# Delta rule in a new order on every engine, with its decays made in the gate stage

## The reference, cut to what matters

```python
qkvz = x @ W_in                              # x after layer norm
b, a = split(x @ W_ba, 2)
q, k, v = silu(causal_conv4(q, k, v))
beta = sigmoid(b);  g = -exp(max(A_log, -2.3)) * softplus(a + dt_bias)
q = l2norm(q) * 64 ** -0.5;  k = l2norm(k)
for each token t:                            # per sequence and head
    S = S * exp(g)
    S = S + k (v - k.T S) * beta
    y = q.T S
y = y * rsqrt(mean(y*y) + 1e-6) * norm_w * silu(z);  out = y @ W_o
```

## Time and profile before

| | |
|---|---|
| three runs | 5923.43, 5942.83, 5943.84 us; median 5942.83 |
| the profiled execution | 5944.53 us, its span 5942.7 us |
| granted TensorE clock, mean | 0.757 |
| TensorE, VectorE, GpSimd, ScalarE busy | 4563.3, 3452.1, 2243.2, 1849.6 us |
| gate stage | about 1475 to 1763 us |
| delta stage | 1763 to about 4960 us, with its start until 1930 |

### The profile page before, as it was taken

One profiled execution on the slowest core, in us unless ns is written; L12 is line 12 of the kernel. 1 busy time (PEld: TensorE's weight loads), 2 busy tenths in 40 slices (PEclk: granted clock), 3 DMA queues, 4 the chain that ended last, 5 costly groups with the idle time before them and its releaser, 6 DMA issues. The chain is left out here.

```text
span 5942.7 us, 161345 instructions
## 1 busy us (share of the span) xinstructions
PE 4563.3 (77%) x65093; PEld 3220.1 (54%) x65093; DVE 3452.1 (58%) x6879; ACT 1849.6 (31%) x3151; POOL 2243.2 (38%) x2773
## 2 busy tenths in 40 slices
PE   7888869997226888888888888888888875887544
PEld 6666634444223666666666666566666654666221
DVE  3444467876225666666666666666666543554577
ACT  0000011111224444444444444444444432333000
POOL 1111100000013666766666666666666651000000
PEclk6555579998556888888888888888888886555777
DMA  0000000000121111111111111111111110000210
GB/s 13 11 14 11 9 25 11 14 11 15 37 62 23 30 32 28 31 30 30 30 28 29 29 32 28 30 30 31 29 30 29 27 27 16 19 19 22 55 32 25
DMA packets 684989, 153.48 MB, mean 26 GB/s; under 512 B 560345, under 2 KB 674721, under 8 KB 683937
## 3 DMA queue, kind: packets, MB, share of 16 engines
q1 hardware_dynamic: 675872, 139.90, 12.1%
q10 hardware_dynamic: 8448, 4.20, 0.2%
HBM read 90.41 MB, written 53.50 MB: 24 GB/s over the span
## 5 line engine op out<-in xcount | busy, mean ns | idle before, releaser
L1604 DVE SCALAR_TENSOR_TENSOR d_acc<-d_xr,d_cq,d_acc 128x512 f32<-128x512 f32 x768 | 591.7, 771 | 164.0 <-ACT d_acc L1277 140.2
L1424 PE MATMUL d_pa<-d_wv,d_hs 128*128 128x512 f32 x1024 | 536.2, 672 | 0.0
L1246 POOL TENSOR_TENSOR d_prod<-d_tblk,d_ablk 128x15 f32<-128x15 f32 (+7 forms) x960 | 426.5, 444 | 114.1 <-DMA d_ablk<-a_blocks 33.8
L1399 PE MATMUL d_pa<-d_hq,d_wqk 128*128 128x259 f32 x1024 | 419.4, 549 | 47.4 <-ACT d_acc L1277 42.0
L1249 POOL TENSOR_TENSOR d_tblk<-d_tblk,d_prod 128x15 f32<-128x15 f32 (+7 forms) x960 | 420.1, 438 | 75.2
L1409 PE MATMUL d_pa<-d_kq 64*64 64x128 f32 x4096 | 182.4, 327 | 291.4 <-DVE d_qk L1620 221.0
L1276 ACT ACTIVATE d_xr<-d_pa 128x518 f32<-128x518 f32 x256 | 154.1, 602 | 767.1 <-PE d_pa L1399 765.5
L1424 PEld LDWEIGHTS d_pa<-d_wv,d_hs 128*128 128x128 f32 x1024 | 227.1, 227 | 241.0 <-issue 229.4
L1223 POOL TENSOR_TENSOR d_nr<-d_n,d_powers 128x32 f32<-128x32 f32 x64 | 347.4, 5428 | 5.9 <-DVE d_n L1734 5.9
L1409 PEld LDWEIGHTS d_pa<-d_kq 64*64 64x64 f32 x4096 | 146.1, 161 | 324.3 <-issue 324.3
L1219 POOL TENSOR_TENSOR d_f<-d_ms,d_mhalf 128x16 f32<-128x16 f32 x64 | 213.6, 3337 | 254.8 <-DVE d_ms L1653 254.8
(11 more groups left out here) (389 smaller groups left out, 10927.0 us busy)
## 6 DMA issues: line engine op xcount, KB each, us to landing
d_hs<-h_t SPq DMA_DIRECT2D x512, 32.0 KB, 1.8
t_blocks<-d_tblk SPq DMA_DIRECT2D x64, 256.0 KB, 2.0
a_blocks<-d_at SPq DMA_DIRECT2D x512, 16.0 KB, 1.8
d_ablk<-a_blocks SPq DMA_DIRECT2D x64, 128.0 KB, 2.1
d_ti<-t_blocks SPq DMA_DIRECT2D x512, 16.0 KB, 1.9
d_tt<-t_blocks SPq DMA_DIRECT2D x512, 16.0 KB, 1.9
d_hq<-h_t SPq DMA_DIRECT2D x16, 259.0 KB, 3.0
a_xt<-in_x SPq DMA_DIRECT2D x16, 256.0 KB, 2.9
```

The costliest lines, as they stand in the source:

```text
L1246: link(pool.tensor_tensor(prod[:, 0:s + 1, 0:n], tblk[:, 0, 0:s + 1, s].unsqueeze(2).to_broadcast([P, s + 1, n]), ablk[:, s, s + 1:SB].uns ...
L1399: last = pe.matmul(pa[:, A + b, 0:QH], wqk[:, col * P:(col + 1) * P], hq[:, n, b, :], start=True, stop=True)
L1424: last = pe.matmul(pa[:, B + m, :], hs[:, u % 2, t, :], wv[:, t, cols(m)], start=(t == 0), stop=(t == TAPS - 1))
L1604: last = dve.scalar_tensor_tensor(out=own, in0=xr[:, e % 2, :, t:t + QT], scalar=cq[:, t, col:col + 1], in1=own, op0=ALU.mult, op1=ALU.add)
```

## The change

*Gate stage.* The rounds are pipelined by hand (`units`, `iteration(p, q)`): in one iteration v the decays of unit v are made, unit v+1 gets its gates, unit v+2 is normalised and unit v+3 loaded; `xt`, `hT` and `out` have two buffers. New: VectorE makes `gu` = g times the mask `due` (4 products of 128x1024 a round), TensorE sums them (8 matmuls of 512 columns into two banks, twice), ScalarE takes 4 Exp of 128x1024 into `dec`, GpSimd masks `dec` in place (2 products of 128x2048), SyncE stores 2 MB a round in `decays`. g itself is no longer stored (`GATES` = 4 x 16).

*Delta stage.* The decays of a chunk are loaded (512 KB) to one of two buffers of `dd`; L1236, L1554, L1355 and L1262 are gone. `kkq` of the first half goes to banks A, of the second to B; VectorE weighs both first in the step. `nr` is a power of 16 columns, and the query's norm goes into `tq`, which is added to the mean square in `ms` (so `f2` and its products go). `t4` for `ti` goes to `pb` bank 0, and its part for `tt` is copied by ScalarE (4 copies, `tt4_ready`) instead of VectorE. The order changes on every engine; on TensorE it is now: ks, kkq(0), kkq(1), conv(0), w4, conv(1), v(0), t4, conv(2), w5, v(1), t5, conv(3), z, solve, turn k (to B), turn o, update, qs, output, turn q (to A), output sums.

```diff
@@ gate_phase, gpsimd
+                if have(p, q + 2):
+                    pool.wait_ge(sem("var_ready"), v + 3)
+                    pool.tensor_tensor(rstd[:, :], ve[:, :], mhalf[:, :], ALU.pow).then_inc(sem("rstd_ready"), 1)
+                if have(p, q):
+                    for c in range(2):
+                        pool.wait_ge(sem("decays"), NC * v + 2 * c + 2)
+                        own = dec[:, q % 2, 2 * c:2 * c + 2, :, :].rearrange("p c h t -> p (c h) t")
+                        pool.tensor_tensor(own, own, due[:, :].unsqueeze(1).to_broadcast([P, 2 * DH, CH]), ALU.mult)\
+                            .then_inc(sem("masked"), 1)
@@ gate_phase, tensor
+                def exponents(c):
+                    pe.wait_ge(sem("gu_ready"), NC * v + c + 1)
+                    wait(pe, sem("decays"), NC * v + c - 1)
+                    for m in range(2):
+                        last = pe.matmul(pe_[:, c % 2, m, :], after[:, :, :].rearrange("p b s -> p (b s)"),
...
@@ gate_phase, vector
+                if now:
+                    products(0)
+                if far:
+                    dve.wait_ge(sem(f"x_loaded{q % 2}"), 32 * (p + (q + 2) // 2 + 1))
...
+                if now:
+                    products(1)
+                    products(2)
+                if then:
...
+                    dve.scalar_tensor_tensor(out=aa[:, :, :], in0=ad[:, :, :], scalar=-1.0, in1=ad[:, :, :],
+                                             op0=ALU.mult, op1=ALU.max).then_inc(sem("aa_ready"), 1)
...
+                if now:
+                    products(3)
@@ delta_phase, sync
+                if have(p, u) and have(p, u + 2):
+                    hold(sem("qk_read"), 2 * i + 2)
+                    load_decays(u % 2, i + 2)
                 if have(p, u + 2):
                     if have(p, u):
                         hold(sem("z_sum"), i + 1)
@@ delta_phase, gpsimd
-                if have(p, u + 2):
-                    n = i + 2
-                    hold(sem(f"gates_loaded{(u + 2) % 4}"), 16 * ((NCH // 4) * p + (u + 2) // 4 + 1))
-                    if not isinstance(n, int) or n > 0:
-                        pool.wait_ge(sem("qk_read"), 2 * n)
-                    pool.tensor_tensor(dd[:, :, :], spread(gt[:, (u + 2) % 4, 1, :], CH),
-                                       upto[:, :].unsqueeze(1).to_broadcast([P, DH, CH]),
-                                       ALU.mult).then_inc(sem("gU_ready"), 1)
+                if have(p, u - 1):
+                    pool.wait_ge(sem("ms_ready"), i)
+                    pool.tensor_tensor(f[:, :], ms[:, :], mhalf[:, :], ALU.pow).then_inc(sem("f_ready"), 1)
@@ delta_phase, tensor
+                    hold(sem("q_squared"), k + 1)
+                    kkq(p, u + 1, 0)
                     if past:
                         hold(sem("o_ready"), i)
-                    elif now:
-                        hold(sem("z_taken"), i + 1)
-                    kkq(p, u + 1, 0)
+                    else:
+                        hold(sem("k_taken"), k + 1)
+                    kkq(p, u + 1, 1)
                 if cv:
                     conv(p, u, 0)
-                if then:
-                    hold(sem("qk_read"), 2 * k + 1)
-                    kkq(p, u + 1, 1)
@@ delta_phase, vector
+                if then:
+                    weigh(p, u + 1, 0)
+                    weigh(p, u + 1, 1)
+                if past:
+                    dve.wait_ge(sem("o_squared"), i)
+                    dve.wait_ge(sem("tq_ready"), i)
...
+                if far:
+                    dve.wait_ge(sem(f"dd_loaded{u % 2}"), 16 * ((NCH // 2) * p + (u + 2) // 2 + 1))
+                    for m in HALVES:
+                        dve.tensor_tensor(dd[:, u % 2, half(m), :], dd[:, u % 2, half(m), :], spread(cc[:, half(m)], CH),
+                                          ALU.mult).then_inc(sem("dd_ready"), 1)
```

More of the change, by code:

```diff
@@ L1100, in _ @@
                 load_gates(s, s)
+            for s in range(2):
+                load_decays(s, s)
             sp.dma_start(wv[:, TAPS - 1, :], w_in[:, 2 * KV:3 * KV]).then_inc(sem("weights"), 16)
@@ L1300, in iteration @@
                 conv = have_conv(p, u)
+                now, past, then, far = have(p, u), have(p, u - 1), have(p, u + 1), have(p, u + 2)
                 if conv:
@@ L1320, in iteration @@
                 if conv:
-                    take_conv(p, u, 3)
-                if have(p, u):
+                    silu_conv(p, u, 2)
+                if then:
+                    act.wait_ge(sem("v_sum"), 2 * k + 2)
+                    silu(v[:, cols(1)], pa[:, B + 1, :]).then_inc(sem("v_taken"), 1)
+                if now:
                     act.wait_ge(sem("t5_sum"), i + 1)
@@ L1395, in conv @@
                     hold(sem(f"h_loaded{n}"), 16 * (p + ((u + 1) // QS + 1) // 2 + 1))
[L1396 removed]
+                    if have(p, u + 1):
+                        hold(sem("qk_read"), 2 * (NCH * p + u + 1) + 1)
                 hold(sem("x_last"), done)
@@ L1467, in iteration @@
                     conv(p, u, 1)
+                if then:
+                    if isinstance(p, int) and not now:
+                        pe.wait_ge(sem("weights_ready"), 1)
+                    hold(sem(f"hs_loaded{(u + 1) % 2}"), 16 * TAPS * 2 * ((NCH // 2) * p + (u + 1) // 2 + 1))
+                    hold(sem("qk_read"), 2 * k + 2)
+                    project_v(p, u + 1, 0)
                 if now:
@@ L1481, in iteration @@
                     conv(p, u, 2)
-                if then:
-                    if isinstance(p, int) and not now:
-                        pe.wait_ge(sem("weights_ready"), 1)
-                    hold(sem(f"hs_loaded{(u + 1) % 2}"), 16 * TAPS * 2 * ((NCH // 2) * p + (u + 1) // 2 + 1))
-                    hold(sem("qk_read"), 2 * k + 2)
-                    project_v(p, u + 1, 0)
                 if now:
@@ L1544, in iteration @@
                     last.then_inc(sem("update"), 1)
+                if now and carried(u):
+                    hold(sem("yT_ready"), i)
+                    against_state(u, queries, pa[:, A:A + 2, :]).then_inc(sem("qs"), 1)
+                if past:
+                    hold(sem("yT_ready"), i)
+                    for j in range(DJ):
+                        last = pe.matmul(pb[:, 0, 0:D], yT[:, j, :], wo[:, j, :], start=(j == 0), stop=(j == DJ - 1))
+                    last.then_inc(sem("out_ready"), 1)
                 if far:
@@ L1551, in iteration @@
                         hold(sem("x_last"), turns(p, u) + CB)
[L1552 to L1565 removed]
+                    hold(sem("kq_ready"), ready_kq(p, u + 2))
+                    turn(u + 2, 1, A).then_inc(sem("q_turned"), 1)
                 if now:
[L1567 removed]
+                    if far:
+                        hold(sem("k_taken"), n + 1)
+                    elif then:
                         hold(sem("z_taken"), k + 1)
+                    else:
+                        hold(sem("o_ready"), i)
                     hold(sem("y_ready"), 2 * i + 2)
```

589 lines of the change are left out of this document (320 added, 269 removed).

## The result

The changed kernel takes 5848.94 us (median of 4 runs, 5842.77 to 5850.60) against 5943.34 us before (4 runs, 5923.43 to 5947.69) on the same chip: a ratio of 0.9851, 95% interval 0.9833 to 0.9869. That is 1.5% faster, where 0.2% was forecast. The range held the time. The forecast's own stretch (5890 to 5975, chance 0.42) did not: the time lies in that of rival 1 (5800 to 5890, chance 0.27). Of the three directions, faster by over 0.5% had been the likeliest (0.40), and it came.

The account below looks back on a forecast made before the run. The prediction took the loop of SyncE's queue and GpSimd's chain as the bound. From 5944.5 us, -74 for the delta stage, +3 for its start and +58 for the gate stage gave 5932 us; range 5820 to 6035.

Parts of the forecast that it names:

- rival 1: Gate and delta stages: GpSimd's masks block less; rounds of 17 us, chain of 15, total 5850 us; chance 0.27.
- The bound: Delta stage: the loop of SyncE's queue and GpSimd's chain of 30 dependent operations sets the step, 47.9 us a round.
- the removed wait of 216.5 us: Delta stage, TensorE's key products: wait for qk_read, 3.5 us a step, not in the loop and so worth nothing.
- Waits taken from the loop: Delta stage: at_ready 0.95, o_ready 0.3 and GpSimd's lateness 1.1 us go; -2.35 us a step.
- load_decays: Delta stage, SyncE's queue: new load ahead of the eight hs loads adds 0.68 us a step, bounds 0.5 and 2.5.
- The chain: Delta stage, GpSimd's 30 operations: 16.0 to 16.2 us beside VectorE's work, +0.45 us a step, bounds -2.5 and +2.5.
- Gate stage: Pipelined rounds of 20.5 us, lengthened by GpSimd's masks shutting out VectorE; stage 346 us, +58, bounds -40 and +85.
- The prediction's -40: Gate stage: lower bound of its term, for rounds of 15 us.
- The bounds of the delta stage: Delta stage: -230 and +95 us around its forecast of -74 us over 62 steps.
- The start of the delta stage: Start of the delta stage: two 512 KB loads put ahead of the weights cost +3 us.
- the signs: Profile: w4 waits 6 to 9 us on ti_clean; gate stage's VectorE products take up to 6 us beside a mask.
- Rival 3: Delta stage: VectorE's two-operand work falls wholly onto GpSimd's chain, 18.1 us, total 6056; chance 0.24 shared with late decays.

Follow-up runs that it names:

- e4: Changed kernel with both halves of the key products in the same banks again; 5844.8 us, ratio 0.9850 to the kernel before.
- e5: Changed kernel with VectorE's products o by f and o by z moved behind the scaling of v, into GpSimd's chain; 5921.0 us, ratio 0.9966 to before.
- e1: Changed kernel with the scores' stores, their hold and the load of ablk moved first in SyncE's step; 5598.0 us, ratio 0.9435 to before.
- e3: Changed kernel with only the decays' load moved behind the load of ablk on SyncE's queue; 5834.6 us, ratio 0.9836 to before.
- e6: Changed kernel with the gate stage's masks made by VectorE instead of GpSimd; 5788.9 us, ratio 0.9741 to before.
- e7: Changed kernel with GpSimd's masks cut to the first of 32 head columns of each operation; 5755.9 us, ratio 0.9688 to before.

## Why the prediction was right or wrong

**The bound: right.** The step follows the loop of SyncE's queue and GpSimd's chain. Shown by e4 (TensorE's wait back, no time), e5 (chain +1.37, step +1.33) and e1. Costing the removed wait of 216.5 us at nothing was right too (e4). The time came out 83 us below the forecast of 5932: the step fell by 2.39 us where 1.2 was forecast (73 us in 61 steps), the gate stage grew by 15 us less, and some 5 us elsewhere went the other way.

**Waits taken from the loop, forecast -2.35, measured -1.8: nearly right.** The waits for `at_ready` and `o_ready` are gone (0.8 and 0.2 by the issues). GpSimd's lateness gave 0.8 instead of 1.1: `ablk` lands 2.07 us after its issue in the round that I read, but in a quarter of the rounds after the change later than 2.4.

**`load_decays`, forecast +0.68: right in size.** The part with gates and decays grew by just this. Not foreseen was that the eight `hs` issues behind it would take 0.48 longer. e3 shows that its removal brings 0.1 to 0.2, not 0.68.

**The chain, forecast +0.45, measured -1.39: the mis-sized term.** 1.84 us a step, 112 us in 61 steps. I placed two filter blocks, the scaling of `v` and the decay of the state into the chain, 7.1 us. A chain of the changed kernel (VectorE and GpSimd):

```profile
3334.35 2.33 DVE L1736 SCALAR_TENSOR_TENSOR d_acc<-d_xr,d_cq,d_acc 128x512 f32<-128x512 f32 x3
3335.38 0.58 POOL L1378 TENSOR_TENSOR d_prod<-d_tblk,d_ablk 128x15 f32<-128x15 f32 x1 [10.03 <-DMA d_ablk<-a_blocks]
...
3340.41 1.32 DVE L1813 TENSOR_TENSOR d_v<-d_v,d_nr 128x1024 f32<-128x1024 f32 x1 [3.74 <-ACT d_v L1414]
3340.73 1.17 POOL L1381 TENSOR_TENSOR d_tblk<-d_tblk,d_prod 128x63 f32<-128x63 f32 x1
3341.97 0.30 POOL L1378 TENSOR_TENSOR d_prod<-d_tblk,d_ablk 128x64 f32<-128x64 f32 x1
...
3343.35 2.33 DVE L1736 SCALAR_TENSOR_TENSOR d_acc<-d_xr,d_cq,d_acc 128x512 f32<-128x512 f32 x3 [1.62 <-ACT d_acc L1402]
3343.53 0.73 POOL L1378 TENSOR_TENSOR d_prod<-d_tblk,d_ablk 128x60 f32<-128x60 f32 x1
...
3347.89 1.22 DVE L1821 TENSOR_REDUCE d_n<-d_sq 128x16 f32<-128x1024 f32 x1 [2.22 <-ACT d_sq L1484]
3348.00 0.26 POOL L1381 TENSOR_TENSOR d_tblk<-d_tblk,d_prod 128x28 f32<-128x28 f32 x1
...
3349.04 0.62 POOL L1384 COPY d_tblk<-d_tblk 128x256 f32<-128x256 f32 x1 [0.17 <-POOL d_tblk L1381]
...
3350.33 1.22 DVE L1832 TENSOR_TENSOR d_state<-d_state,d_gt 128x1024 f32<-128x1024 f32 x1
```

Here the decay of the state (L1832) comes after the chain and its turned copy (L1384), half of the first filter block lies ahead of it, and all that VectorE does in the chain's last 3.2 us is a sum over one tile (L1821), beside which GpSimd's operation takes its usual 0.26 us. Over all 64 chains, summing the overlaps, products with two inputs in SBUF cover 5.2 us of a chain; before they covered 6.8, for `o` by `f`, `o` by `z` and the decay of the state often lay in it. I had given the kernel before too little of this and the changed one too much. The exchange rate was near: a fit of the chain's operations on their shape and on what covers them gives 0.67 to 0.69 us lost for each us of filter and 0.8 to 0.9 for the other products, with 8.0 us for the 30 alone and 0.08 between them, 10.3 in all, where I had 11. 6.8 - 5.2 = 1.6 us at these rates are 1.1 to 1.4, nearly all of the measured gain.

**Gate stage, forecast +58, measured +43.1: mechanism right, size off.** Rounds take 19.2 us, not 20.5; the masks take 4.5 us each when nothing holds them, where I had 5.1, twice a round. That GpSimd's masks shut out VectorE is shown by the rows and runs of e6 and e7. They cost 91 us, and without them the pipeline is 48 us shorter than the old stage. The prediction's -40 for rounds of 15 us does not follow from its own terms: 18 + 15 x 15 + 20 = 263, which is -25.

**Other sums.** The bounds of the delta stage, -230 and +95, don't follow from those of its terms either; added end to end these give -270 and +164. The start of the delta stage, forecast +3, came out at +4.2. Of the signs, `w4` waits 4.9 us a step and not 6 to 9 (8.8 is the longest), and VectorE's products reach 5.5 us beside a mask, as expected.

**Rival 1 named the time (5850) but not the way there.** It had rounds of 17 us and a chain of 15; they are 19.2 and 14.2. The two errors have opposite signs, and that its sum meets the time is luck. Rival 3 was the right term with the wrong sign; e5 shows that placing can lengthen the chain, to 15.6 us and not 18.1.

## What to carry to other kernels

Find the loop that closes last, with its issues and not only its waits, before costing an edit by the wait that it removes. What an edit makes early is worth something only once the queue that takes it comes earlier as well: here, moving one block of SyncE's stream gave 251 us in the changed kernel and nothing in the one before. And of instructions on VectorE beside a chain on GpSimd, count by name those that read two tiles of SBUF, and order the others, with PSUM inputs or sums over one tile, into that time.

## What the runs showed of the hardware

A VectorE product with one input in PSUM costs GpSimd next to nothing: the state addition (L1837) covered 14.0 us of the chains and the sums of L1821 40.9, and the fit gives either at most 0.05 us lost per us. The Trainium skill (SBUF — State Buffer, Who interferes with whom) says that VectorE with at most one SBUF input, outside its two-port modes, does not contend with GpSimd; this agrees. It also says that whoever is first holds the ports for the whole instruction, which the gate stage shows to the last tenth of a us.

The same lock holds a tiny instruction with a single SBUF input, though: L991, a `tensor_scalar` of 4 columns. Its row in the changed kernel, and in e7 (ns min/median/max):

```profile
L991 DVE TENSOR_SCALAR g_ve<-g_mv x16: 170/3137/4405, 1476.9 to 1742.9; 128x4 f32<-128x4 f32 x16
```

```profile
L991 DVE TENSOR_SCALAR g_ve<-g_mv x16: 169/170/171, 1475.5 to 1670.7; 128x4 f32<-128x4 f32 x16
```

3.1 us instead of 0.17, beside the masks: 10 of the 16 end when a mask does. The same section of the skill names `tensor_scalar` among the instructions that can take the two-port modes, which would be the reason; no run here separates it.

The granted clock rose with the gate stage's pipelining: 0.50 before, 0.76 after, 0.85 in e6 and 0.89 in e7, in the windows above, so more of the stage ran at 2.4 GHz and less at 1.2. The 256 records of L915 took 175.3 us in the changed kernel and 140.5 in e7. How much of the 91 us of e7 is the clock's, no run here separates.
